# The last of four batches, written out behind the loop without the preparation of a following batch

## What is computed

```python
q = (x @ Wq.T + bq).reshape(Bx, Lx, H, hd)          # k_, v likewise
scores = jnp.einsum('bqhd,bkhd->bhqk', q, k_) * scale + bias[None, None, None, :]
attn = jax.nn.softmax(scores, axis=-1)
ctx = jnp.einsum('bhqk,bkhd->bqhd', attn, v).reshape(Bx, Lx, Dx)
y = x + (ctx @ Wo.T + bo)
a = layernorm(x + layernorm(y) * gamma + beta)
xq = quantize_activations(a @ H)                    # 4 bits, scale by row
out = layernorm(a + jnp.einsum('bsi,oi->bso', xq, ternary(weight)))
```

## Time and profile before

| | |
|---|---|
| median of 3 executions | 5490.9 us (5487.32 to 5498.97) |
| the profiled execution's own time | 5480.82 us |
| its span | 5478.7 us |
| PE busy | 5073.5 us, 93% |
| POOL, DVE, ACT busy | 57%, 63%, 48% |
| mean granted clock of PE | 0.974 |

### The profile page before, as it was taken

One profiled execution on the slowest core, in us unless ns is written; L12 is line 12 of the kernel. 1 busy time (PEld: TensorE's weight loads), 2 busy tenths in 40 slices (PEclk: granted clock), 3 DMA queues, 4 the chain that ended last, 5 costly groups with the idle time before them and its releaser, 6 DMA issues.

```text
span 5478.7 us, 91809 instructions
## 1 busy us (share of the span) xinstructions
PE 5073.5 (93%) x25449; PEld 2498.7 (46%) x25449; DVE 3428.0 (63%) x5964; ACT 2602.5 (48%) x4910; POOL 3130.0 (57%) x1103
## 2 busy tenths in 40 slices
PE   6999999998899999999889999999888999999988
PEld 3444444543444444444444444444444444444434
DVE  4575657566675665757656565756675756565756
ACT  0454545453454554545345454545444545454534
POOL 1464646565465665646546464656664646565654
PEclk7999999999999999999989999999999999999999
DMA  4414142313413223141331414132233141314134
GB/s 111 91 36 93 36 82 47 76 36 90 110 36 62 55 48 76 36 93 36 104 79 36 93 36 90 39 64 58 51 94 81 36 91 38 76 36 93 36 78 122
DMA packets 260526, 366.80 MB, mean 67 GB/s; under 512 B 17298, under 2 KB 106162, under 8 KB 260019
## 3 DMA queue, kind: packets, MB, share of 16 engines
q1 hardware_dynamic: 260018, 360.67, 29.9%
HBM read 217.39 MB, written 33.55 MB: 46 GB/s over the span
## 4 chain that ended last, share of the span: by engine, by line
PE 74%; DMA 11%; issue 4%; POOL 4%; DVE 2%; ACT 2%; SPq 2%; POOLq 0%; ACTq 0%; DVEq 0%
PE ps_m L469 21%; PE ps_s L484 19%; PE ps_o L509 16%; DMA qst<-lo 6%; PE ps_z L489 5%; PE ps_m L455 4%; DMA xk<-in_xT_dram 3%; PE ps_m L423 3%; PE ps_m L429 3%; SPq L285 1%; POOL prob L995 1%; POOL prob L999 1%; PE ps_s L429 1%; PE ps_s L423 1%; ACT prob L665 1%
## 5 line engine op out<-in xcount | busy, mean ns | idle before, releaser
L784 DVE TENSOR_REDUCE umax<-ps_m 128x1 f32<-128x512 f32 x4160 | 2564.8, 683 | 775.8 <-PE ps_m L469 775.7
L665 ACT ACTIVATE prob<-ps_s 128x512 f32<-128x512 f32 x4096 | 2125.3, 601 | 1652.3 <-PE ps_s L484 1441.7
L969 POOL TENSOR_TENSOR acc<-acc,prob 128x2048 f32<-128x2048 f32 x512 | 2345.7, 4581 | 461.1 <-ACT prob L665 437.3
L484 PE MATMUL ps_s<-qst,kst 99*128 99x512 f32 x4096 | 1696.9, 430 | 137.6 <-ACT prob L665 74.9
L469 PE MATMUL ps_m<-kst,qst 97*128 97x512 f32 x4160 | 1726.6, 423 | 34.9 <-DMA qst<-lo 34.9
L484 PEld LDWEIGHTS ps_s<-qst,kst 99*128 99x128 f32 x4096 | 761.7, 190 | 1217.5 <-ACT prob L665 656.4
L509 PE MATMUL ps_o<-prob,vst 128*32 128x512 f32 x8192 | 1094.7, 606 | 0.0
L469 PEld LDWEIGHTS ps_m<-kst,qst 97*128 97x128 f32 x4160 | 793.4, 191 | 475.6 <-DVE umax L784 330.7
L969 POOL TENSOR_TENSOR acc<-prob 128x2048 f32<-128x2048 f32 x64 | 292.9, 4577 | 674.8 <-ACT prob L665 674.8
L953 POOL TENSOR_TENSOR obuf<-obuf,zinv 128x512 f32<-128x512 f32 x64 | 82.1, 1282 | 910.6 <-DVE zinv L797 910.6
L764 DVE SCALAR_TENSOR_TENSOR lo<-ps_m,bias,hi 128x512 fp32r<-128x512 f32 x122 | 91.6, 751 | 691.2 <-ACT hi L633 368.5
(11 more groups left out here) (105 smaller groups left out, 2421.5 us busy)
## 6 DMA issues: line engine op xcount, KB each, us to landing
xk<-in_xT_dram SPq DMA_DIRECT2D x74, 1024.0 KB, 9.0
xq<-in_xT_dram SPq DMA_DIRECT2D x67, 1024.0 KB, 8.8
kst<-hi SPq DMA_DIRECT2D x144, 256.0 KB, 10.6
qst<-hi SPq DMA_DIRECT2D x132, 256.0 KB, 5.6
kst<-lo SPq DMA_DIRECT2D x72, 256.0 KB, 10.3
wq<-in_wT_dram SPq DMA_DIRECT2D x67, 256.0 KB, 9.2
qst<-lo SPq DMA_DIRECT2D x66, 256.0 KB, 6.8
ctxT_dram<-obuf SPq DMA_DIRECT2D x64, 256.0 KB, 2.6
```

Source lines behind the costliest of these rows:

```text
L484: nc.tensor.matmul(ps_s[:, (i * HG * NKC + HG * c + h) % NSB, :], kst[i // NQB % 2][0:RALL, h, c * P:(c + 1) * P], qst[i % 2][0:RALL, h, : ...
L665: nc.scalar.activation(prob[:, c % NPB, h, :], ps_s[:, (i * HG * NKC + HG * c + h) % NSB, :], ACT.Exp, scale=SCALE).then_inc(ex, 1)
L784: nc.vector.tensor_reduce(umax[:, m, kb:kb + 1], ps_m[:, u % NMB, :], AX.X, ALU.max).then_inc(mred, 1)
L969: nc.gpsimd.tensor_tensor(acc[:], a, prob[:, c % NPB], ALU.add).then_inc(padd, 1)
```

## The change

The body of the loop becomes a function `batch(b, last)` on every engine. The loop runs over three batches, and the fourth is written out behind it with `last=True` and a constant `b`. In it these are left out: the keys and values in block 12 with their loads; the maxima units of block 15 with their transposition, copies and reductions; the queries in blocks 14 and 15 with their stacking and loads; the four key quarters in the token stage; and `next_weights`. Waits that counted this work count less, at the end of SP's program too.

```diff
-            def tokens(b):
+            def tokens(b, last):
...
-                    sp.wait_ge(k_stk[t], (b * NG + NG + 1) * (2 * NSTK))
-                wait_alone(sp, q_stk, (b * NBLK + NBLK + 2) * NSTK, passed)
+                    sp.wait_ge(k_stk[t], (b * NG + NG + (0 if last else 1)) * (2 * NSTK))
+                wait_alone(sp, q_stk, (b * NBLK + NBLK + (0 if last else 2)) * NSTK, passed)
...
-                        if 0 < s - KEY_STEP <= NQB:
+                        if not last and 0 < s - KEY_STEP <= NQB:
                             keys_quarter(bb * NG + NG + 1, bb, NG + 1, s - KEY_STEP - 1)
-                next_weights(NG + 1)
+                if not last:
+                    next_weights(NG + 1)
...
-            with sp.Fori(0, NB) as b:
+            def batch(b, last):
                 for i in range(NBLK):
                     with block_of(sp, b, i) as n:
                         s = i // NQB
-                        if i > 0 and i % NQB == 0:
+                        if i > 0 and i % NQB == 0 and not (last and i == NBLK - NQB):
                             keys((n >> 2) + 1, (n >> 4) & (NB - 1), s + 1)
-                        maxima(n + 1, i + 1)
+                        if not (last and i == NBLK - 1):
+                            maxima(n + 1, i + 1)
                         wait_alone(sp, sc, (n + 1) * (HG * NKC), passed)
-                        queries(n + 2, (n >> 4) & (NB - 1), i + 2)
+                        if not (last and i >= NBLK - 2):
+                            queries(n + 2, (n >> 4) & (NB - 1), i + 2)
                         store_context(n, i, (n >> 2) & (NS - 1))
-                tokens(b)
+                tokens(b, last)
+
+            with sp.Fori(0, NB - 1) as b:
+                batch(b, False)
+            batch(NB - 1, True)
...
-            sp.wait_ge(wkv_ld, (NS + 3) * 32)
+            sp.wait_ge(wkv_ld, (NS + 1) * 32)
...
-            def attend(n, i):
+            def attend(n, i, last):
...
-                        for u in units_at[c][h]:
+                        for u in () if last and i == NBLK - 1 else units_at[c][h]:
                             unit(u, n + 1, i + 1, (n >> 2) + 1 if i % NQB == NQB - 1 else None)
                     if c == NKC - 2:
-                        maxima_to_rows(n + 1)
-                        queries(n + 2)
+                        if not (last and i == NBLK - 1):
+                            maxima_to_rows(n + 1)
+                        if not (last and i >= NBLK - 2):
+                            queries(n + 2)
```

More of the change, by code:

```diff
@@ L572, in tokens @@
                         t = s - KEY_STEP
-                        if 0 <= t < NQB:
+                        if not last and 0 <= t < NQB:
                             stage = bb * NG + (NG + 1)
@@ L610, in _, with batch @@
             keys(1, 0)
-            with pe.Fori(0, NB) as b:
+            def batch(b, last):
                 for i in range(NBLK):
@@ L616, in _ @@
                                 score(n, 0, 0, h, head=True)
-                        if i > 0 and i % NQB == 0:
+                        if i > 0 and i % NQB == 0 and not (last and i == NBLK - NQB):
                             keys((n >> 2) + 1, n)
-                        attend(n, i)
-                tokens(b)
+                        attend(n, i, last)
+                tokens(b, last)
                 batch_done(pe, c_st, b, passed)
+            with pe.Fori(0, NB - 1) as b:
+                batch(b, False)
+            batch(NB - 1, True)
         @block.scalar
@@ L742, in _, with batch @@
             keys(1, 1, 0)
-            with act.Fori(0, NB) as b:
+            def batch(b, last):
                 for i in range(NBLK):
@@ L748, in _ @@
                                 exponential(n, 0, 0, h)
-                        if i > 0 and i % NQB == 0:
+                        if i > 0 and i % NQB == 0 and not (last and i == NBLK - NQB):
                             keys((n >> 2) + 1, i // NQB + 1, n)
-                        attend(n, i, n >> 2)
-                tokens(b)
+                        attend(n, i, n >> 2, last)
+                tokens(b, last)
                 batch_done(act, c_st, b, passed)
+            with act.Fori(0, NB - 1) as b:
+                batch(b, False)
+            batch(NB - 1, True)
         @block.vector
@@ L854, in tokens @@
                         k = s - KEY_STEP - 1
-                        if 0 <= k < NQB:
+                        if not last and 0 <= k < NQB:
                             stage = bb * NG + (NG + 1)
@@ L933, in _, with batch @@
             keys(1, 1, 0)
-            with dve.Fori(0, NB) as b:
+            def batch(b, last):
                 for i in range(NBLK):
                     with block_of(dve, b, i) as n:
-                        if i > 0 and i % NQB == 0:
+                        if i > 0 and i % NQB == 0 and not (last and i == NBLK - NQB):
                             keys((n >> 2) + 1, i // NQB + 1, n)
-                        maxima(n + 1)
-                        queries(n + 2, i + 2)
+                        if not (last and i == NBLK - 1):
+                            maxima(n + 1)
+                        if not (last and i >= NBLK - 2):
+                            queries(n + 2, i + 2)
                         inverse_sums(n)
-                tokens(b)
+                tokens(b, last)
                 batch_done(dve, c_st, b, passed)
+            with dve.Fori(0, NB - 1) as b:
+                batch(b, False)
+            batch(NB - 1, True)
         @block.gpsimd
@@ L1026, in _, with batch @@
             pool.sem_inc(cbias, 1)
-            with pool.Fori(0, NB) as b:
+            def batch(b, last):
                 for i in range(NBLK):
@@ L1034, in _ @@
                             normalise(n, i)
-                tokens(b)
+                tokens(b, last)
                 batch_done(pool, c_st, b, passed)
+            with pool.Fori(0, NB - 1) as b:
+                batch(b, False)
+            batch(NB - 1, True)
 def kernel(L0_attn_x, L0_attn_band_importance, L0_attn_Wq, L0_attn_bq, L0_attn_Wk, L0_attn_bk, L0_attn_Wv, L0_attn_bv,
```

34 lines of the change are left out of this document (18 added, 16 removed).

## The result

The changed kernel takes 5370.65 us (median of 4 executions, 5359.28 to 5375.65), against 5490.52 us for the kernel before in the same comparison: a ratio of 0.9776, 95% interval 0.9757 to 0.9796, or 120 us less. Forecast were 5420 us, 70.5 us less.

The account below looks back on a forecast made before the run. PE was taken as the bound while the maxima units run, POOL next. 32.4 + 16.0 + 0.7 + 10 + 7.4 + 4.0 = 70.5 us off 5490.9 gives 5420 us, range 5406 to 5436 (5407 to 5435 by the bounds).

Parts of the forecast that it names:

- the one on code: Whole program: text gets longer, but the loop body is streamed anew in each pass already; costed at nothing.
- rival 4: Written-out batch: straight copy starves the sequencers, slower from 16 stalls of 4.62 us on, up to 5716 us; chance 0.03.
- Block 12: Last batch, block 12: dropping the next batch's keys and their loads saves 32.4 us, bounds 31 and 34.
- Block 14: Last batch, block 14: dropping the query projection gains 2.5 us, not 3.6, as the maxima copy becomes late.
- Block 15: Last batch, block 15: without maxima units and projection some 48.5 us; gain 16.0 including block 14's 2.5, bounds 12 and 17.
- Seam into the token stage: Last batch, after block 15: context store lands sooner without the useless loads; gain 0.7 us, bounds 0 and 2.
- The last token steps: End of last batch: without key quarters steps take 8.7, 8.7 and 7.8 us; gain 10 us to the store, bounds 4 and 14.
- The end: Behind the last store's issue: 3.2 us remain of 10.6; gain 7.4 us, bounds 6 and 8.
- The third seam: Between third and fourth batch: fall-through instead of back-edge shortens PE's issue; gain 4.0 us, between 0 and 4.6.
- Rival 3: Third seam: leaving the loop costs what the back-edge costs, 5424 us; counted inside the forecast's chance of 0.82.
- Rival 1: Block 15: small gaps make PE's clock swing to half; only 48 us saved, 5443 us; chance 0.07.
- Rival 2: Block 15: units hidden anyway, POOL and ACT hold its present length; 57 us saved, 5434 us; chance 0.06.

Follow-up runs that it names:

- e1: Fourth batch written out behind the loop with a constant b, nothing left out, against the kernel before; ratio 0.9913, 48 us faster.
- e9: e1 with SP's loop kept over four batches, so only the four other engines are written out; ratio 0.9914 to the kernel before.
- e13: Kernel before with 4000 small matmuls added after PE's loop, result unused; ratio 1.0147, which contains the added matmuls.
- e14: Kernel before with 11000 small matmuls added after PE's loop, result unused; ratio 1.0551, which contains the added matmuls.
- e2: Changed kernel with all four batches written out instead of only the fourth; ratio 0.9785 to the kernel before.
- e10: e1 with only SP's fourth batch written out, the four other engines keeping their loops over four; ratio 0.9990 to the kernel before.
- e11: e7 with three idle matmuls on PE in each of token steps 14 to 18 of the last batch; ratio 0.9700 to the kernel before, 5321 us.
- e7: e2 with rows of the transposed x 8320 elements apart instead of 8192; ratio 0.9725 to the kernel before, 5330 us.
- e8: Changed kernel with block 15's maxima units and the block 14 query projection they read left in; ratio 0.9811 to the kernel before.
- e12: Meant to test text that is never executed; gave no result, and its edit is not described.

## Why the prediction was wrong, step by step

**The step that failed is the one on code.** It asked whether a longer text costs fetches, found that it is streamed anew in each pass, and costed it at nothing. That is right for the engines: rival 4, the stalls of a straight copy, didn't come, and the plain blocks of the written-out batch are shorter, not longer. It is wrong for the kernel: e1, e9, e13 and e14 show that more text of PE (or of the four engines) alone shortened the blocks with keys by 2 to 3 us each in a loop that isn't touched (in e2, with the most text, they gained only 1.4), 26 us in the nine of batches 1 to 3 of the changed kernel. What the runs put in place of the nothing is key loads of x that land in 7.7 us and not 9.0. Blocks 4 and 8 of its batch 4 gained 12.8 us, from this and from the constants of the next paragraph together. The prediction compared only the part of the program that the diff changes, and took the rest as fixed.

**Waits against constants were overlooked.** The prediction has no term for "a constant b". 5422 register instructions fewer in a batch are worth 0.3 us in each plain block (3.4 us in ten) and, by e1, some 2.3 us in each block with keys (93.4 in its last batch against 95.8 in its loop), although there the batches may differ for other reasons too.

**Block 12.** Forecast 32.4, measured 32.7; in e1, with waits against constants, the dropped keys are worth 93.6 - 63.8 = 29.8. The window of both blocks contained what it was taken to contain; the other 2.9 us would have come without the drop, by the sooner loads and the constants.

**Block 14.** Forecast 2.5, measured 2.1. As forecast the copy of the maxima became the late one: PE's first scores of block 15 wait 1.00 us for it.

**Block 15.** Forecast a length of about 48.5 us, with PE and POOL meeting (its own sum gives 48.7 to 49.0); measured 50.0. POOL's additions come every 4.69 us and not every 4.6, and the last column sums, behind PE's wait, take 1.94 us instead of about 1. PE's own chunk turned out shorter than the 2.77 us read between two blocks, 2.61, and lies hidden behind POOL; its wait for ACT inside a group of scores, read between two blocks, is 0.22 us in the written-out batch (e1 and e9 too) and 0.38 in the loops of these kernels and of e10, so it goes with the written-out text, whose waits are against constants.

**Seam into the token stage.** The context store lands in 2.41 us instead of 3.32; forecast 0.7, measured 0.9.

**The last token steps.** Forecast 8.7, 8.7 and 7.8 us; measured, from the starts of the scaling at 5323.31, 5331.93, 5340.66 and 5348.12: 8.6, 8.7 and 7.5. The granted clock is 0.65 from 5326 us on, where about 0.5 was forecast. e11 confirms the reason. Seam, token steps and end together gave 18.3 us; forecast were 18.1.

**The end.** The last stores land in 2.0 us, and the span ends 2.9 us behind the issue of the last; forecast 3.2.

**The third seam.** Forecast 4.0 us by the shorter issue, which measured 4.62 before and 0.93 after. It stands for 3.7; the whole seam gave 8.6, the rest being a store that lands 0.8 us sooner and key quarters and a token stage that are shorter by the same unforeseen means. Rival 3 is out: over the three seams of each of the 15 traces, every back-edge of PE has 4.4 to 5.3 us of issue, and every fall-through has 0.70 to 0.93, or 2.35 us of a chain over ACT in kernels with all batches written out (e2, e7, e11). The Trainium skill (Runtime: NRT & Kernel Launch, Instruction fetch mechanics) has the rule for it, that a taken branch out of the window in hand waits for a fetch; the traces agree, with 4.62 us before and 0.93 after, though they show the issue and not the fetch.

**Rival 1, the clock in block 15.** It fell out: the granted clock of the window from 5134 to 5184 us is 0.97. PE is busy 43.66 of these 50 us, 87% and not the 70% that the rival assumed. The swing of the clock that the Trainium skill (TensorE: Matmul & The Clock Gate, A second HAM failure mode: psum-queue depth-cycling) tells of another kernel did not appear here, with gaps under 1 us in each chunk. **Rival 2** was refuted by e8.

**The range.** Its bounds were those of the steps in the sum. Added up they give 52 to 79.6 us saved, so 5411 to 5439 us and not the 5407 to 5435 that the prediction states; 5370.65 lies outside both. No bound stood for the eleven blocks with keys and the three token stages that the change leaves as they are.

## What stays open

Shown is that more text, at unchanged instructions in the loop, changes the landing of the key loads of x, and that the padded rows change it in the same way and not in addition. Also shown is that it is the packets in the blocks with keys that get shorter, not those of the query loads. That the common cause is where x, or something else that is read at the same time, lies in memory, is argued from this and not shown: no run moved x alone by a known amount that mattered (8 KB did not), and e2, with the longest text, has slow loads. Another traffic of the DMA engines, or the moment at which loads and stacking copies meet, is not excluded. Why 8320 helps where 8192 is slow is open as well, and so is what text that is never executed would do (e12, meant for this, gave no result). e13 and e14 rest on one trace each.

## What to carry to other kernels

When a change makes a program's text longer or shorter, transfers in stretches where the DMA engines are full can move by some per cent anywhere in the kernel, as here; give the range a term for it, and test with a copy that has the text and not the change. A strided load from memory at a power-of-two row distance is worth trying with padded rows where it meets other traffic: here 30 us in one kernel, 34 in another, nothing in a third. In a kernel whose waits are computed from loop registers, writing the loop out removes those instructions and most of the issue at each back-edge; and where an engine's work is dropped, look who was just below it: in block 15 POOL took 50.0 of the 62.4 us that PE had held.

## What was not expected of the hardware

Matmuls placed behind the last instruction of interest, in a program otherwise the same, made the 5250 us ahead of them 23 to 30 us faster. The same 260018 packets took 1638 us of each DMA engine in one kernel and 1578 in another with the same work. Three idle matmuls in each of five steps raised PE's granted clock from 0.59 to 0.94 in a stretch of 36 us and made it 4.4 us shorter, although PE did more. PE's wait for ACT between two groups of scores was 0.38 us in the loop, with semaphore values computed in registers, and 0.22 in written-out text, with constants. Where the chain stayed on PE, a fall-through cost 0.70 to 0.93 us of issue, a back-edge 4.4 to 5.3.
